# Softmax denominators as a further column of the values, and outputs scaled by POOL, in one attention stage of a twelve-stage kernel

## What is computed

```python
sparse_mask = ...            # about 0.2 of the 512 tokens in each of two groups are kept
q = (x @ Wq + bq).reshape(B, S, nh, hd)
k = (x @ Wk + bk).reshape(B, S, nh, hd) * mask
v = (x @ Wv + bv).reshape(B, S, nh, hd) * mask
scores = jnp.einsum("bqhd,bkhd->bhqk", q, k) * scale
attn = jax.nn.softmax(scores, axis=-1)
out = jnp.einsum("bhqk,bkhd->bqhd", attn, v).reshape(B, S, H)
return out @ Wo + bo
```

## Time and profile before

| | us |
|---|---|
| median of 3 runs | 2013.42 |
| lowest, highest | 2007.55, 2013.45 |
| the profiled execution | 2014.1 |
| its span | 2012.3 |
| attention, from its first maxima to its last instruction on DVE | 715.4 to 801.1 |
| mean granted clock of TensorE, share of full speed | 0.918 |

### The profile page before, as it was taken

How to read it: one execution, slowest core, us unless ns; L and a number is a source line. 1 busy time by engine, 2 the same in 40 slices (tenths; PEclk the granted TensorE clock), 3 DMA queues, 4 the chain that set the end, 5 groups by cost and what they waited for, 6 DMA issues and landing times. The chain is left out here.

```text
span 2012.3 us, 30205 instructions
## 1 busy us (share of the span) xinstructions
PE 1719.6 (85%) x11138; PEld 1408.7 (70%) x11138; DVE 1467.1 (73%) x3097; ACT 1224.4 (61%) x2445; POOL 900.6 (45%) x872
## 2 busy tenths in 40 slices
PE   6899479988992667897889998898999999988899
PEld 4799258857991356775688885676777777766788
DVE  7888577579885766775777667677877877867665
ACT  3488347635870378228723435888888887887443
POOL 0577531006857200303722210476787777778411
PEclk9999779989995789788989998999999999999899
DMA  8588315016963100000020100000000000000111
GB/s 302 158 274 266 92 48 162 29 50 192 288 224 100 47 1 2 1 1 0 1 93 1 52 14 2 21 22 19 24 22 19 25 22 22 22 14 1 52 39 34
DMA packets 74320, 138.63 MB, mean 69 GB/s; under 512 B 11444, under 2 KB 52532, under 8 KB 73140
## 3 DMA queue, kind: packets, MB, share of 16 engines
q1 hardware_dynamic: 63412, 107.23, 16.3%
q0 software_dynamic: 10752, 29.37, 5.1%
HBM read 112.45 MB, written 24.12 MB: 68 GB/s over the span
## 5 line engine op out<-in xcount | busy, mean ns | idle before, releaser
L79 PE MATMUL ps<-work_r 128*128 128x256 f32 (+2 forms) x1392 | 289.0, 301 | 12.7 <-ACT work L87 4.1
L79 PE MATMUL ps<-H_r,wt_r 128*128 128x512 f32 (+1 forms) x732 | 290.2, 436 | 11.1 <-DVE wt_r L91 8.1
L79 PE MATMUL ps<-wt,work 128*128 128x256 f32 (+2 forms) x1144 | 238.4, 384 | 16.5 <-POOL work L91 6.9
L91 DVE TENSOR_TENSOR work<-work,ps 128x512 f32<-128x512 f32 (+4 forms) x314 | 177.6, 566 | 95.9 <-ACT work L87 59.8
L87 ACT ACTIVATE work<-ps 128x512 f32<-128x512 f32 (+3 forms) x355 | 168.2, 497 | 122.4 <-PE ps L79 99.9
L79 PEld LDWEIGHTS ps<-work_r 128*128 128x128 f32 (+1 forms) x1392 | 221.3, 187 | 23.9 <-ACT work_r L87 6.2
L79 PEld LDWEIGHTS ps<-wt,work 128*128 128x128 f32 (+1 forms) x1144 | 179.3, 209 | 43.7 <-ACT work L87 10.1
L99 DVE SCALAR_TENSOR_TENSOR wt<-ps,wt 128x511 f32<-128x511 f32 (+2 forms) x234 | 174.4, 747 | 35.4 <-ACT wt L87 29.8
L79 PE MATMUL ps<-ering_r,work_r 128*128 128x256 f32 (+1 forms) x806 | 193.4, 306 | 1.0 <-ACT work L87 1.0
L145 POOL DMA_INDIRECT work<-Hd,work x128 | 124.7, 974 | 152.9 <-DVE work L91 62.6
L91 POOL TENSOR_TENSOR work<-work 128x256 f32<-128x256 f32 (+2 forms) x164 | 139.5, 852 | 116.0 <-ACT work L87 88.0
(11 more groups left out here) (224 smaller groups left out, 4247.4 us busy)
## 6 DMA issues: line engine op xcount, KB each, us to landing
ering<-in_moe_w SPq DMA_DIRECT2D x85, 624.0 KB, 5.4
ye<-work SPq DMA_DIRECT2D x64, 256.0 KB, 3.8
wt<-in_ssd_wg SPq DMA_DIRECT2D x64, 128.0 KB, 2.2
ye<-early SPq DMA_DIRECT2D x1, 4096.0 KB, 14.6
wt<-in_ssd_wg SPq DMA_DIRECT2D x8, 512.0 KB, 3.6
Hd<-H SPq DMA_DIRECT2D x16, 128.0 KB, 1.7
wt<-in_ret_fc SPq DMA_DIRECT2D x2, 1024.0 KB, 12.4
work<-Hd,work POOLq DMA_INDIRECT x128, 4.4
```

The source lines that it names most:

```text
L79: self.last = self.e.matmul(o, l, r, start=start, stop=stop, skip_group_check=True)
L91: self.last = self.e.tensor_tensor(o, a, b, op)
```

## The change

The values get a seventeenth column in each head: 1 in every slot, and 385 in slot 127, which is an empty one and stands for itself and the 384 tokens without a slot. The product `av` thus gives the denominator of each head and token in row 16 of the head's 32 rows. The exponentials make no sums, the step `scale` is gone, and two steps are new between `av` and `wo`:

- `sums`: PE multiplies a constant 128 x 128 matrix `own` by `oT` (one matmul with 512 columns) into a bank of its own, which holds each head's denominator in all of its 32 rows. DVE takes the reciprocal of the bank (128 x 512) into `rec`.
- `norms`: POOL multiplies `oT` by `rec` in place.

`wo` waits for POOL. Of the four copies of `PT`, ACT keeps r = 0 and 2, and DVE takes r = 1 and 3. `oT` has four buffers in place of two. DVE writes the seventeenth column by four small operations ahead of the first tile, and SP loads `own`. POOL's additions of `bo` stand between its products, from the fourth tile on. The activation tables are loaded twice in the stage and no longer four times: the first square roots come behind all exponentials.

```diff
--- before.py
+++ after.py
@@ -593,7 +593,7 @@
             todo, live, begun = [], [], set()
 
             def tile(t):
-                for step in ("scores", "scale", "PT", "av", "wo"):
+                for step in ("scores", "PT", "av", "sums", "norms", "wo"):
                     todo.append((step, t))
                     yield
                 if t % 2 == 0:
@@ -1722,7 +1722,7 @@
         M4.qT = W(4, 1024)
         M4.col, M4.ncol, M4.sgn, M4.coded, M4.ties, M4.eqb, M4.msk, M4.pre, M4.pos = (W(2, 4) for _ in range(9))
         M4.eqi = W(2, 4).bitcast(U32)
-        M4.ms, M4.nb, M4.vcol = W(2), W(2), W(2)
+        M4.ms, M4.nb, M4.vcol, M4.count, M4.own = W(2), W(2), W(2), W(1), W(128)
         M4.vbc, M4.hs = W(2, 128), W(2, 256)
         keep_top, top["wt"] = top["wt"], mark
         M4.kT = carve("wt", (4, 2, 128))
@@ -1732,9 +1732,10 @@
         M4.P = [carve("wt", (4, 128)) for _ in range(10)] + [a.rearrange("p (m n) -> p m n", m=4) for a in flat[:2]]
         M4.PT = [a.rearrange("p (m n) -> p m n", m=4) for a in flat[2:]]
         top["wt"] = keep_top
-        M4.mx, M4.dn, M4.rc = ([W(16) for _ in range(4)] for _ in range(3))
-        M4.oT = [W(4, 128) for _ in range(2)]
-        s_lm = sig("before_in")
+        M4.mx = [W(16) for _ in range(4)]
+        M4.rec = [W(4, 128) for _ in range(2)]
+        M4.oT = [W(4, 128) for _ in range(4)]
+        s_lm, s_own = sig("before_in"), sig("own_in")
 
         def pe_attn(pe, si):
             m_ = M4
@@ -1792,24 +1793,30 @@
                 elif s[0] == "PT":
                     for r in range(4):
                         b = ps.take(pe, "PT", t, r)
-                        pe.wait_ge(V, "P", t, r)
+                        pe.wait_ge(A, "P", t, r)
                         for m in range(4):
                             pe.tr(b[:, cols(m)], m_.P[(4 * t + r) % 12][:, m, :], ident)
                         pe.then_inc(PE, "PT", t, r)
                 elif s[0] == "av":
                     b = ps.take(pe, "av", t)
                     pe.wait_ge(V, "v", t // 4)
-                    pe.wait_ge(A, "PT", t, 3)
+                    pe.wait_ge(A, "PT", t, 2)
+                    pe.wait_ge(V, "PT", t, 3)
                     for m in range(4):
                         for r in range(4):
                             pe.mm(b[32 * r:32 * r + 32, cols(m)], m_.vv[t // 4][:, 4 * m + r, :], m_.PT[(4 * t + r) % 8][:, m, :],
                                   True, True)
                     pe.then_inc(PE, "av", t)
+                elif s[0] == "sums":
+                    b = ps.take(pe, "sums", t)
+                    pe.wait_ge(A, "oT4", t)
+                    pe.wait_ge(s_own, "in")
+                    pe.mm(b, m_.own, m_.oT[t % 4].rearrange("p m n -> p (m n)"), True, True).then_inc(PE, "sums", t)
                 elif s[0] == "wo":
                     b = ps.take(pe, "wo", t)
-                    pe.wait_ge(A, "oT4", t)
+                    pe.wait_ge(G, "oT", t)
                     for m in range(4):
-                        pe.mm(b[:, 0:256], m_.oT[t % 2][:, m, :], wts["attn_wo"][:, m, :], m == 0, m == 3)
+                        pe.mm(b[:, 0:256], m_.oT[t % 4][:, m, :], wts["attn_wo"][:, m, :], m == 0, m == 3)
                     pe.then_inc(PE, "wo", t)
 
         def a_attn(a, si):
@@ -1833,24 +1840,19 @@
                 a_step(a, s)
                 t = s[-1]
                 if s[0] == "scores":
-                    mx, dn, rc = m_.mx[t % 4], m_.dn[t % 4], m_.rc[t % 4]
+                    mx = m_.mx[t % 4]
                     for r in range(4):
                         b, p = ps.of("score4", t, r), m_.P[(4 * t + r) % 12]
                         a.wait_ge(V, "mx", t, r)
                         if t >= 3:
                             a.wait_ge(PE, "PT", t - 3, r)
-                        if t >= 4:
-                            a.wait_ge(V, "rc", t - 4)
                         for m in range(4):
                             h = 4 * r + m
-                            a.act(p[:, m, :], b.ap[:, cols(m)], ACT.Exp, scale=0.25, bias=mx[:, h:h + 1],
-                                  accum_out=dn[:, h:h + 1]).then_inc(A)
+                            a.act(p[:, m, :], b.ap[:, cols(m)], ACT.Exp, scale=0.25, bias=mx[:, h:h + 1])
+                            a.then_inc(A, "P", t, r)
                         a.frees(b)
-                    if t >= 4:
-                        a.wait_ge(V, "P", t - 4, 3)
-                    a.act(rc, mx, ACT.Exp).then_inc(A, "sums", t)
                 elif s[0] == "PT":
-                    for r in range(4):
+                    for r in (0, 2):
                         b = ps.of("PT", t, r)
                         a.wait_ge(PE, "PT", t, r)
                         if t >= 2:
@@ -1860,9 +1862,9 @@
                 elif s[0] == "av":
                     b = ps.of("av", t)
                     a.wait_ge(PE, "av", t)
-                    if t >= 2:
-                        a.wait_ge(PE, "wo", t - 2)
-                    a.act(m_.oT[t % 2], b.ap.rearrange("p (m n) -> p m n", m=4), ACT.Copy).then_inc(A, "oT4", t).frees(b)
+                    if t >= 4:
+                        a.wait_ge(PE, "wo", t - 4)
+                    a.act(m_.oT[t % 4], b.ap.rearrange("p (m n) -> p m n", m=4), ACT.Copy).then_inc(A, "oT4", t).frees(b)
 
         def v_attn(v, si):
             m_ = M4
@@ -1928,6 +1930,12 @@
                 v.wait_ge(PE, "k", m)
                 v.stt(m_.kT[:, m, :, :], b.ap[:, 0:256].rearrange("p (a n) -> p a n", a=2), wts["attn_bk"][:, m:m + 1],
                       m_.vbc, ALU.add, ALU.mult).then_inc(V, "k", m).frees(b)
+            v.ts(m_.count, pidx[:, 0:1], 126.5, ALU.is_ge, 384.0, ALU.mult).then_inc(V)
+            v.wait_ge(V)
+            v.ts(m_.count, m_.count, 1.0, ALU.add).then_inc(V)
+            v.wait_ge(V)
+            for h in range(2):
+                v.copy(m_.vv[h][:, :, 16], bc(m_.count, [128, 16])).then_inc(V)
             for h in range(2):
                 b = ps.of("v", h)
                 v.wait_ge(PE, "v", h)
@@ -1941,25 +1949,29 @@
                 t = s[-1]
                 if s[0] == "scores":
                     mx = m_.mx[t % 4]
-                    if t >= 4:
-                        v.wait_ge(A, "sums", t - 4)
                     for r in range(4):
                         b = ps.of("score4", t, r)
+                        if t >= 4:
+                            v.wait_ge(A, "P", t - 4, r)
                         v.wait_ge(PE, "score4", t)
                         v.red(mx[:, 4 * r:4 * r + 4], b.ap.rearrange("p (m n) -> p m n", m=4), ALU.max).then_inc(V)
                         v.wait_ge(V)
                         v.ts(mx[:, 4 * r:4 * r + 4], mx[:, 4 * r:4 * r + 4], 0.0, ALU.max, -0.25, ALU.mult)
                         v.then_inc(V, "mx", t, r)
-                elif s[0] == "scale":
-                    dn, rc = m_.dn[t % 4], m_.rc[t % 4]
-                    v.wait_ge(A, "sums", t)
-                    v.stt(dn, rc, 384.0, dn, ALU.mult, ALU.add).then_inc(V)
-                    v.wait_ge(V)
-                    v.rcp(rc, dn).then_inc(V, "rc", t)
-                    v.wait_ge(V)
-                    for r in range(4):
-                        p = m_.P[(4 * t + r) % 12]
-                        v.tt(p, p, bc(rc[:, 4 * r:4 * r + 4].unsqueeze(2), [128, 4, 128]), ALU.mult).then_inc(V, "P", t, r)
+                elif s[0] == "PT":
+                    for r in (1, 3):
+                        b = ps.of("PT", t, r)
+                        v.wait_ge(PE, "PT", t, r)
+                        if t >= 2:
+                            v.wait_ge(PE, "av", t - 2)
+                        v.copy(m_.PT[(4 * t + r) % 8], b.ap.rearrange("p (m n) -> p m n", m=4))
+                        v.then_inc(V, "PT", t, r).frees(b)
+                elif s[0] == "sums":
+                    b = ps.of("sums", t)
+                    v.wait_ge(PE, "sums", t)
+                    if t >= 2:
+                        v.wait_ge(G, "oT", t - 2)
+                    v.rcp(m_.rec[t % 2], b.ap.rearrange("p (m n) -> p m n", m=4)).then_inc(V, "rec", t).frees(b)
                 elif s[0] == "wo":
                     b = ps.of("wo", t)
                     v.wait_ge(PE, "wo", t)
@@ -1967,18 +1979,24 @@
                     v.tt(X[:, t, :], X[:, t, :], b.ap[:, 0:256], ALU.add).then_inc(V, "X", si, t).frees(b)
 
         def g_attn(g, si):
-            for a in M4.vv:
+            m_ = M4
+            for a in m_.vv:
                 g.memset(a, 0.0).then_inc(G, "kv0")
             for s in order[si]:
                 if s[0] == "av":
                     t = s[1]
                     g.wait_ge(V, "H", si, t)
                     g.tt(X[:, t, :], X[:, t, :], wts["attn_bo"], ALU.add).then_inc(G, "bo", t)
+                elif s[0] == "norms":
+                    t, o = s[1], m_.oT[s[1] % 4]
+                    g.wait_ge(V, "rec", t)
+                    g.tt(o, o, m_.rec[t % 2], ALU.mult).then_inc(G, "oT", t)
 
```

(2 more changed lines are left out.)

## The result

| | us | runs |
|---|---|---|
| kernel before, median (lowest, highest) | 2012.59 (2004.68, 2016.33) | 20 |
| changed kernel, median (lowest, highest) | 2018.32 (2010.85, 2024.3) | 20 |
| ratio changed to before, 95% interval | 1.0034 (1.0020 to 1.0047) | |

The change makes the kernel slower by 0.34%, some 6.8 us (the two medians are 5.7 us apart).

What follows compares the result with a forecast made beforehand. ACT and the way back over PE and DVE were taken to bind, not DVE's scaling. Terms +0.1 - 0.8 - 2.6 + 4.1 + 7.7 = +8.5 us on 2014.1 gave 2022.6; forecast 2019.5 to 2027, range 2015.5 to 2029.5.

Steps and rivals of the forecast that it cites:

- the first rival: PE's clock holds in the early tiles, so the 4.1 us fall away: +4.4, 2018.5 us; chance 0.20.
- The reciprocal: On DVE, 128 x 512: 3.4 us, 3.3 until the next instruction starts, from sizes 1, 8 and 16.
- The exponentials: On ACT, without sums: 0.26 us apart, sixteen make 4.2 us, 1.3 less than before.
- The period: Spacing of tiles: stays at 8.7 us by the loop over ACT and PE, with DVE's loop at 8.1.
- the rival that DVE binds the tiles: DVE's 8.1 us binds the tiles; faster by 5 us with the clock and the quick reciprocal; chance 0.03.
- the beginning: Tiles 0 and 1: tile 2's maxima come 12.9 us after tile 0's, 0.8 less than before.
- the five periods: Spaces from tile 2's to tile 7's maxima: five of 8.7, 43.5 us, 2.6 less than before.
- half clock: PE's `av` and scores of early tiles slowed at three of four places: 1.4, 1.1 and 1.6, 4.1 us in all.
- The end: From tile 7's maxima to the stage's end: 33.6 us against 25.9, +7.7, four long reciprocals in a row.
- Eight steps: On DVE, the reciprocal costs 4.35 us, with DVE's loop at 9.2: 2028.8 us; chance 0.10.
- More half clock: On PE, all six `av` and scores pairs and the last `wo` slowed: +7.8, 2030.4 us at the most; chance 0.12.
- A quick reciprocal: On DVE, it takes 0.61 us and PE binds the end, 30.2 us: 2019.2, with the clock 2015; chance 0.07.

Runs made afterwards that it cites:

- exp_sums: Changed kernel with each exponential's sum put back, into a buffer nobody reads: stage 105.91 us against 92.47; 2056.10 us in one run.
- copy_rcp: Changed kernel with a plain DVE copy of the same size in place of the reciprocal: stage 86.44 us against 92.47; 2040.02 us in one run.
- late: Changed kernel with everything of a tile behind its scores one iteration later: stage 88.59 us against 92.47; 2012.13 us in one run.
- warm: Changed kernel with idle-time matmuls on PE ahead of `av` of tiles 0 to 3: stage 88.85 us against 92.47; 2045.67 us in one run.
- b_warm: Kernel before with idle-time matmuls on PE ahead of the transposes of tiles 0 to 6: stage 83.11 us against 85.75; ratio 0.9986.
- bo_first: Changed kernel with POOL's eight bias additions all ahead of its products: stage 94.57 us against 92.47; 2023.02 us, once.
- pt_act: Changed kernel with all four copies of `PT` on ACT, none on DVE: stage 102.67 us against 92.47; 2050.81 us, once.
- late_warm: The late kernel with idle-time matmuls on PE ahead of the last transposes of tiles 0 to 5: stage 88.37 us; ratio 1.0018 to before.
- late_copy: The edits of late and copy_rcp together, on the changed kernel: stage 77.96 us against 92.47; 2027.92 us in one run.

## Why the prediction was right, point by point

The forecast was 2022.6 us, 8.5 above the profiled execution, and slower with a chance of 0.71. Measured are 6.8 us by the ratio and 6.7 in the stage. The whole, 2018.32, lies in the range of 2015.5 to 2029.5, but 1.2 us below the forecast's own 2019.5 to 2027. The number alone is the one of the first rival, 2018.5, which was wrong in its mechanism. Three things bring it there: the sum was 1.8 us too high for the stage, the kernel before has a median of 2012.59 over 20 runs, 1.5 below the execution from which I had counted, and the two medians are 1 us closer than the two stages.

- **The reciprocal.** Worked out from three small sizes: 3.4 us, 3.3 until the next starts. Measured: 3.35 and 3.27. The line through 8 and 16 elements holds up to 512: 3348 less 253, over 496, is 6.24 ns an element. The repeat count of 8 that the Trainium skill states in "VectorE: DVE Perf Modes" (First, the fixed hardware budget) had led to an estimate of 4.4 us, as a factor on the time; the trace doesn't agree with it as such a factor, and the measurement decides.
- **The exponentials.** 0.26 apart was said, 0.25 measured. exp_sums shows that the difference was the read of the sums.
- **The period.** 8.7 was said, 8.57 measured at full clock. The loop is the one named: maxima to first exponential 0.93, exponentials 4.02, copies and PE's start 1.30, `av` 1.01, scores to maxima 1.31 (765.50 back to 756.93). exp_sums lengthens it one for one and copy_rcp leaves it alone, so the rival that DVE binds the tiles is out. Where POOL's addition holds up DVE it is 8.82, which the prediction didn't have. What the lighter exponentials gave, the place of `av` took back, and late shows that place: 7.1 us without it, as long as no reciprocals run.
- **The beginning and the clock.** I put the beginning 0.8 us shorter, the five periods 2.6 shorter, and half clock at 4.1 us on top. warm separates these: 12.56 us for tiles 0 to 2 at full clock (I had 12.9) and 3.6 us net for half clock. It fell at three places, as said, but the sizes were 1.9, 0.7 and 1.3 us, where I had 1.4, 1.1 and 1.6. That they add up to 3.9, near my 4.1, is in part luck. The sum of these terms was +0.8, measured -0.2 us. One reading was wrong: I put the table load of 1.28 us into the five spaces before the change. It starts at 776.58, behind tile 7's maxima at 775.23, so it lies in the end. The 2.6 us that these spaces had above five periods were half clock: b_warm brings them down from 46.14 to 42.84. The sum took the measured total, so its number isn't hurt, but the kernel before had its own loss by the clock, which I never set against the 4.1.
- **The end.** 33.6 was said, 32.83 measured, with DVE busy 31.3 of 32.9 us. The surplus of 0.8 us is the largest error of a single term. Up to the last `wo` the list was right to 0.1 us: said was its end at 28.2 behind tile 7's maxima, measured the last addition at 28.26 (802.58 less 774.32), right behind that `wo`. That is in part luck, as errors cancelled: the copies of tile 7 didn't have to wait for PE, which saved 0.6 us, and each `nb` beside a product of POOL took 1.7 us instead of 1.1. The surplus lies behind the last `wo`: 5.4 us were said for the last additions, norm steps and turns, and they took 4.6.
- **The rivals.** That the clock holds: half clock did come. Eight steps: no. More half clock: not in this profile, but its last `wo` at half clock did come in bo_first (1.7 us), and in part in pt_act, late and late_warm. A quick reciprocal: copy_rcp played it, and here a step failed. I had said that the end would be bound by PE at 30.2 us. It was 26.91. The last `wo` ended 22.6 us behind the maxima of tile 7 (823.99 less 801.43), not 25.2. Products `wo` behind each other take 1.73 to 1.83 us to the next row instead of 2.0, and transposes that don't wait for DVE 1.80 instead of 2.4 (808.69 to 810.49). Behind the last `wo` there are 4.3 us, not 5. The price of the reciprocals is therefore 5.9 us, not 3.4, and without them the change would have lost only 0.7 us in the stage.

What I had not seen is how much the order is worth: late_copy's 77.96 us are 8.5 less than copy_rcp's, in the same work. With the reciprocals it is worth less, 3.9 us (late for changed).

## What to carry to other kernels

Before an operation is moved, ask where its result is late: of eight long operations on one engine the first four were free, as the tiles' loop ran over other engines, and the last four cost 5.9 us where the pipeline ran empty, because they then stood in a row. The length of an operation that isn't in the trace was read here from three smaller sizes on one line, and it held to 0.1 us. To judge a change of 0.3% read the one stage it touches and many executions: the two profiled spans had the sign wrong.

## What the runs showed of the hardware

**Two engines on SBUF.** DVE's small operation with one source in SBUF and its result there (128 x 4) takes 0.17 us, and 0.41 or 0.42 when POOL adds two SBUF tiles at that time (747.51, 766.23, 775.04 in the changed kernel; POOL's additions start 0.24 to 0.26 us ahead of each). `nb`'s operation of 128 x 256 takes 0.41 alone and 1.12 or 1.11 beside POOL's product (788.47 and 798.68; POOL 788.17 and 798.38). In both cases DVE ends within 0.15 us of POOL's end. The reductions and reciprocals that read PSUM took 0.69 and 3.35 us throughout. bo_first takes POOL away from the first kind, and it is gone. Not every operation from SBUF is held: beside the same products of POOL a reciprocal of 128 x 1 took its usual 0.15 us (788.29) and the statistics of 128 x 256 their 0.41 or 0.42 (782.50 and 793.57). The Trainium skill has both sides of this: "GPSIMD Engine Reference", 1. Specifications, says that GpSimd shares its SBUF interfaces with VectorE, with contention for instructions in a mode that uses two ports or with two SBUF inputs, and "VectorE: DVE Perf Modes", Mode 2×_2P, that an fp32 operation with one source in SBUF uses both ports and one from PSUM can't. The trace agrees: 0.24 us more for the small and 0.7 for the large, both of the kind that combines one SBUF source with scalars, and none for those from PSUM.

**Sums in an activation.** They cost 0.09 us each on ACT at 128 x 128 (0.344 instead of 0.252 apart), by a row of its own in exp_sums.

**TensorE's clock.** In the kernel before and in the changed one it fell to half behind gaps in which PE did little, and products that fill these gaps kept it at 1.00. That was worth 3.6 us of 92 in the changed kernel and 2.6 of 86 in the kernel before (3.3 up to tile 7's maxima). In the order of late it was worth 1.3 us from tile 2 to 7, where DVE binds most spaces, and 0.2 in the stage. One place has no fixed clock: the last `wo` of the end. In seven profiles PE idles 3.07 or 3.08 us and makes two transposes ahead of it. It took 1.90 us in three (changed, exp_sums, warm) and 2.74 to 3.62 us in four (pt_act, bo_first, late, late_warm).
